# Projecting v for two head groups at once, half of the tokens per job, in a fused attention and mixture-of-experts block

## The chip, the cores and the metric

The kernel runs on one core of one Trainium2 chip. The metric is the device time of one execution in microseconds; 509.33 us is the median of three runs before the change.

## What is computed

There are four batches of 512 tokens with 256 features. The reference, cut to what matters:

```python
def xattn(q, k, v, wq, wk, wv, wo):            # 16 heads of 64, window of 64 keys back
    qh, kh = rope(heads(q @ wq.T)), rope(heads(k @ wk.T))
    vh = heads(v @ wv.T)
    scores = where(window_mask, qh @ kh.T * 64 ** -0.5, -1e30)
    return merge(softmax(scores) @ vh) @ wo.T

x = x + tanh(g_xattn) * xattn(layernorm(x), ctx, ctx, wq, wk, wv, wo)
x = x + tanh(g_ffn) * ffn(layernorm(x), ...)   # 2 shared experts, 16 routed, top 4
```

All large products are made in three float32r products each: every operand is split into a rounded part and a rest (`h` and `l`), and `h*h + h*l + l*h` is summed in PSUM.

## The kernel before

**Units and steps.** Attention is cut into 16 units: unit u is batch u // 4 with the head group g = u % 4 of four heads. A unit has four steps, one per head, so step c is head c % 4 of unit c // 4; 64 steps in all. The list `steps` gives for each step the jobs that are done beside its scores, softmax and transposes, and every engine walks the same list in its own queue. In unit u the q and k of unit u + 1 are projected in steps 4u and 4u + 1, its v in step 4u + 2, and in steps 4u + 1 and 4u + 3 the probabilities are transposed, two heads a time. Job `("v", n)` is the projection of v for unit n, so it stands in step 4n - 2, and ahead of two steps of unit n - 1. The experts follow behind the 64 steps, from about 300 us on.

**Inside TensorE's queue**, an even step begins with the scores of two heads (L1312), goes on with `values` (L1343, probabilities times v, for the pair of heads that was transposed last), and then does its jobs. An odd step has four transposes (L1324) of one head, its jobs, and four transposes of the next. `values(p)` belongs to unit p // 2 and stands in step 2p + 4; the first for unit u therefore stands in step 4u + 4, which is the first step of unit u + 1.

**The v job.** TensorE makes v for four tiles of 128 tokens. Each tile has six products (two halves of the contraction, three products each) with the transposed context as stationary operand and 256 columns of the weight `wh`/`wl` as moving operand, so a job is 24 matmuls of 256 columns into the two PSUM banks of a ring. ScalarE copies both banks (128x1024, L665) to `v_al`, half of which is used for odd, half for even units. SyncE then runs `shift_values`: because a window of 128 keys starts 64 tokens before its block of queries, a second copy `v_sh`, moved by 64 tokens, is made with two DMAs inside SBUF (L369, L370). `values` reads `v_al` for odd blocks of 64 queries and `v_sh` for even ones, and waits for both DMAs through the semaphore `v_in`.

**SyncE's queue** issues all DMAs in the order of `steps`. Behind `shift_values` of an odd unit n stands, in batches 1 and 2 (units 4 and 8, so n = 5 and n = 9), the job `in_scale` (L448): a 256 KB broadcast from DRAM of the scale of the next batch's layer norm into `idle`. GpSimd's job `scale_a` (L540), one step later, waits for it.

**GpSimd's queue** does, besides, the normalisation of the probabilities (`divide`, L521) ahead of the transposes, and half of the rotary embedding (L499 and L502 for q, L508 and L513 for each half of k).

**The weights.** `wh` and `wl` hold 18 slots of 512 floats per partition. The v weights of groups 0 to 3 stand in slots 1, 5, 8 and 12. From the last batch on, expert weights are loaded into slots whose attention weights are done with (`wait_slot_free`).

Of the kernel before, what the change touches and what calls it, by code (L numbers as in the profile page):

```python
# [22 lines left out]
P = 128  # L23
B, L, D = 4, 512, 256
# [40 lines left out]
def build(nc, x_d, xt_d, ctx_d, gx_d, gf_d, w_d, e_d, rw_d, cos_d, sin_d, mask_d, ident_d, out_d):  # L65
    with ExitStack() as ctx:
# [3 lines left out]
        def sem(name):  # L70
# [25 lines left out]
        rw_parts = sb("rw_parts", [P, KC, 2, NR], F32R)  # L96

        sizes = dict(swap=(2, 2, L), qT=(2, 2, L), kT=(2, 2, W + L), idle=(1, 1, L), late=(2, TT, P), spare=(1, 1, 256),
                     v_al=(2, TT, GD), v_sh=(2, TT, GD))
        arena = sb("arena", [P, sum(int(np.prod(s)) for s in sizes.values())])  # L100
        cuts, at = {}, 0
        for name, (a, b, c) in sizes.items():
# [2 lines left out]
        idle = cuts["idle"][:, 0, 0, :]  # L105
        swap = cuts["swap"]
        qT, kT = cuts["qT"], cuts["kT"]
        v_al, v_sh = cuts["v_al"], cuts["v_sh"]
        gate_bc = arena[:, 0:NR * L].rearrange("p (e n) -> p e n", e=NR)
        sneg_a = sb("sneg", [P, 2, TT, P])  # L110
        sneg = [sneg_a[:, 0, :, :], sneg_a[:, 1, :, :], cuts["late"][:, 0, :, :], cuts["late"][:, 1, :, :]]
# [194 lines left out]

            return j if j < 2 else j - B + 2

        def fillings(u):

            return u // 2 + 1

        def side(j):

# [13 lines left out]
        def wait_slot_free(eng, i):  # L328

            if i >= NE:  # L330
                kind, g = ORDER[slot(i)]
                eng.wait_ge(y_pe if kind == "y" else v_pe, (B - 1) * GROUPS + g + 1)

        def gated_parts(n):

# [18 lines left out]
        def _(sp):  # L354
# [8 lines left out]
                sp.wait_ge(c_lo, b + 1)  # L363
                sp.dma_start(craw[:, :, :], ctx_d[b]).then_inc(in_ctx, 16)

            def shift_values(u):

                sp.wait_ge(v_out, u + 1)
                sp.dma_start(v_sh[W:P, u % 2, :, :], v_al[0:W, u % 2, :, :]).then_inc(v_in[u % 2], 16)  # L369
                sp.dma_start(v_sh[0:W, u % 2, 1:TT, :],  # L370
                             v_al[W:P, u % 2, 0:TT - 1, :]).then_inc(v_in[u % 2], 16)

            def move(dst, blocks, done):

# [223 lines left out]
        def _(act):  # L598
# [45 lines left out]
            def do(job):  # L644
                kind, n = job
                if kind == "w":
                    act.wait_ge(in_raw[n % RAW], 16 * (n // RAW + 1))
                    wait_slot_free(act, n)
                    act.activation(wh[:, slot(n), :], raw[:, n % RAW, :], ACT.Copy).then_inc(w_hi, 1)
                elif kind == "ctx" and n == 0:  # L650
                    for kc in range(KC):
                        act.wait_ge(in_ctx0[kc], 16)
                        act.activation(xTh[1][:, kc, :], craw[:, kc, :], ACT.Copy).then_inc(c_hi, 1)
                elif kind == "ctx":
                    act.wait_ge(in_ctx, 16 * n)
                    act.wait_ge(v_pe, GROUPS * n)
                    act.activation(xTh[1][:, :, :], craw[:, :, :], ACT.Copy).then_inc(c_hi, 1)
                elif kind == "xT":
                    round_bank_pair(xTh[side(n)], job, xT_pe, xT_hi)
                elif kind == "v":  # L660
                    act.wait_ge(v_pe, n + 1)
                    if n >= 2:
                        act.wait_ge(oT_pe, 2 * (n - 1))
                        act.wait_ge(v_in[n % 2], 32 * (fillings(n) - 1))
                    act.activation(v_al[:, n % 2, :, :].rearrange("p t d -> p (t d)"),  # L665
                                   both_banks(job)[:, :, :].rearrange("p a n -> p (a n)"),
                                   ACT.Copy).then_inc(v_out, 1)
                elif kind == "expert":
                    expert(n)
                elif kind == "rexp":  # L670
                    act.wait_ge(r_sub, n + 1)
                    act.activation(lexp[:, :, :], lex[:, :, :], ACT.Exp).then_inc(r_exp, 1)
                elif kind == "xhi":
                    X = side(B + n)
                    act.wait_ge(xn_moved, 256 * (n - 1))
                    act.wait_ge(up_pe, NE * (n - 1))
                    act.wait_ge(r_pe, n - 1)
                    act.activation(xTh[X][:, :, :], xnT, ACT.Copy).then_inc(xT_hi, 1)
                elif kind == "xhi_d":
                    act.wait_ge(x_shifted, n - 1)  # L680
                    act.wait_ge(qk_pe[0], GROUPS * n + 1)
                    act.activation(xTh[0][:, :, :], xd, ACT.Copy).then_inc(xT_hi, 1)
                elif kind in ("norm_a", "norm_b"):
                    normalise(n, kind)
# [440 lines left out]
        def _(pe):  # L1125
# [79 lines left out]
            def do(job):  # L1205
# [16 lines left out]
                elif kind in "qk":  # L1222
                    b, g = divmod(n, GROUPS)
                    i = PIECE_OF[kind, g]
                    weights(i)
                    if kind == "q":
                        pe.wait_ge(xT_lo, b + 1)
                    else:
                        pe.wait_ge(c_lo, b + 2)
                    X = 0 if kind == "q" else 1  # L1230
                    for half in range(2):
                        for kc in range(KC):
                            last = product(two[half], [cols(i, kc * D + half * P, P)],
                                           [(xTh[X][:, kc, :], xTl[X][:, kc, :])],
                                           start=kc == 0, stop=kc == KC - 1)
                        if (kind, n) == ("q", 0) or half:
                            last.then_inc(qk_pe["qk".index(kind)], 1)
                elif kind == "v":
                    b, g = divmod(n, GROUPS)
                    i = PIECE_OF["v", g]  # L1240
                    weights(i)
                    pe.wait_ge(c_lo, b + 2)
                    for t in range(TT):
                        last = product(two[t // 2][:, (t % 2) * GD:(t % 2 + 1) * GD],
                                       [(xTh[1][:, kc, t * P:(t + 1) * P],
                                         xTl[1][:, kc, t * P:(t + 1) * P]) for kc in range(KC)],
                                       [cols(i, kc * D, D) for kc in range(KC)])
                    last.then_inc(v_pe, 1)
                elif kind == "y":
                    i = PIECE_OF["y", n % GROUPS]  # L1250
                    weights(i)
                    pe.wait_ge(oT_lo, 2 * (n + 1))
                    for t in range(TT):
                        last = product(two[t // 2][:, (t % 2) * D:(t % 2 + 1) * D],
                                       [(oTh[:, j, t * P:(t + 1) * P], oTl[:, j, t * P:(t + 1) * P])
                                        for j in range(2)],
                                       [cols(i, j * D, D) for j in range(2)])
                    last.then_inc(y_pe, 1)
                elif kind == "r" and n in FULL_ROUTER:
                    pe.wait_ge(xn_moved, 256 * (n - 1))  # L1260
                    for kc in range(KC):
                        for t in range(TT):
                            last = pe.matmul(two[0][QUAD * t:QUAD * t + NR, 0:P], rw[:, kc, :],
                                             xnT[:, kc, t * P:(t + 1) * P], start=kc == 0, stop=kc == KC - 1)
                    last.then_inc(r_pe, 1)
                elif kind == "r":
                    pe.wait_ge(rw_lo, 1)
                    pe.wait_ge(xT_lo, B + n + 1)
                    X = side(B + n)

                    for kc in range(KC):
                        for part in (xTh[X], xTl[X]):
                            last = pe.matmul(two[0][0:2 * NR, :], rw_parts[:, kc, :, :].rearrange("p a e -> p (a e)"),
                                             part[:, kc, :], start=kc == 0 and part is xTh[X],
                                             stop=kc == KC - 1 and part is xTl[X])
                    last.then_inc(r_pe, 1)
# [50 lines left out]
            def values(p):  # L1327
# [1 line left out]
                u, pair = divmod(p, 2)  # L1329
                pe.wait_ge(p_out, 2 * p + 2)  # L1330
                if pair == 0:
                    pe.wait_ge(v_out, u + 1)
                    pe.wait_ge(v_in[u % 2], 32 * fillings(u))
                if p:
                    pe.wait_ge(oT_lo, p)
                else:
                    pe.wait_ge(pool_init, 1)
                for blk in range(L // W):
                    t, e = divmod(blk, 2)
                    v = v_al if e else v_sh  # L1340
                    for h in range(2):
                        head = 2 * pair + h
                        last = pe.matmul(psO[h * DH:(h + 1) * DH, blk * W:(blk + 1) * W],  # L1343
                                         v[:, u % 2, t, head * DH:(head + 1) * DH],
                                         pT[:, (2 * p + h) % 4, t, e * W:(e + 1) * W],
                                         start=True, stop=True)
                last.then_inc(oT_pe, 1)
# [109 lines left out]
```

## Time and profile before

| | |
|---|---|
| median of three runs | 509.33 us (509.26 to 509.49) |
| the profiled execution, its own time | 508.84 us |
| its span in the trace | 507.1 us |
| TensorE busy | 496.7 us, 98% |
| VectorE, ScalarE, GpSimd busy | 358.2, 310.9, 267.3 us |
| granted TensorE clock, mean | 0.999 |

The busy time of an engine is the union of its instructions. Matmuls overlap each other in the trace by their fill and drain, so what a matmul costs is read from the distance between the starts of two, and not from its duration. A unit of attention takes about 17.5 us in the middle of the run. GpSimd's 53% is a mean over a first part in which it is nearly always busy and the experts, where it hardly works.

### The profile page before, as it was taken

To read this page: it belongs to the slowest core of one execution; us is meant where nothing else is said; L and a number is where in the kernel's file an instruction comes from. 1 tells how busy PE (TensorE), PEld (TensorE's weight loads), DVE (VectorE), ACT (ScalarE), POOL (GpSimd) and SP (SyncE) were. 2 spreads that over 40 slices of the span, in tenths; PEclk is the share of its full clock that TensorE was granted. 3 is DMA by queue.
4 is the path that set the end of the run, shared out by engine and by line. 5 is a ranking of instruction groups with operands and counts; after the bars stand their busy time and mean duration, and the time that the engine had idled before them with its cause. 6 is when DMAs were issued, how large, how long until landed. Compare 5 with 4: busy or idle time off the path is not lost.

```text
span 507.1 us, 14396 instructions
## 1 busy us (share of the span) xinstructions
PE 496.7 (98%) x5426; PEld 417.6 (82%) x5426; DVE 358.2 (71%) x1159; ACT 310.9 (61%) x861; POOL 267.3 (53%) x206
## 2 busy tenths in 40 slices
PE   8998999999999999999999999999999999999997
PEld 5778888889988998888888788777878887888885
DVE  6989858665787667768877768786657565745454
ACT  5595785656766665865767765766456545644442
POOL 4999999899997999997888511001000100000000
PEclk9999999999999999999999999999999999999999
DMA  8462124121212210220221146315812680256021
GB/s 268 121 202 80 44 67 135 44 80 38 57 67 71 71 38 24 59 59 23 59 59 27 35 160 247 95 25 145 276 16 31 172 248 10 32 148 238 1 34 49
DMA packets 49363, 46.36 MB, mean 91 GB/s; under 512 B 29936, under 2 KB 32368, under 8 KB 49296
## 3 DMA queue, kind: packets, MB, share of 16 engines
q1 hardware_dynamic: 49296, 45.46, 31.2%
q8 instruction: 43, 0.70, 0.6%
q14 instruction: 24, 0.20, 0.2%
HBM read 32.72 MB, written 2.24 MB: 69 GB/s over the span
## 4 chain that ended last, share of the span: by engine, by line
PE 76%; POOL 13%; DVE 5%; issue 4%; DMA 1%; ACT 1%; SPq 0%; DVEq 0%; POOLq 0%; ACTq 0%
PE ring L1131 54%; PE psS L1131 10%; PE psO L1343 5%; POOL arena L508 4%; PE psT L1324 4%; PE psS L1312 3%; POOL arena L513 3%; POOL prob L521 2%; POOL wl L529 2%; DVE arena L1026 1%; DVE wl L946 1%; POOL arena L502 1%; DVE arena L859 1%; DMA raw<-in_w 1%; POOL arena L499 1%
## 5 line engine op out<-in xcount | busy, mean ns | idle before, releaser
L1131 PE MATMUL ring<-xTh,wh 128*128 128x512 f32 x268 | 108.2, 404 | 0.5 <-DVE lex L888 0.2
L1131 PE MATMUL ring<-xTh,wl 128*128 128x512 f32 x268 | 105.3, 393 | 0.0
L1131 PE MATMUL ring<-xTl,wh 128*128 128x512 f32 x268 | 105.1, 392 | 0.0
L632 ACT ACTIVATE oTh<-prob 128x512 fp32r<-128x512 f32 x64 | 40.4, 631 | 54.3 <-PE ring L1131 26.8
L521 POOL TENSOR_TENSOR prob<-prob,rinv 128x512 f32<-128x512 f32 x62 | 66.8, 1078 | 12.6 <-DVE rinv L1036 12.4
L929 DVE TENSOR_TENSOR oTl<-prob,oTh 128x512 fp32r<-128x512 f32 x64 | 44.1, 689 | 37.1 <-ACT oTh L632 36.7
L555 POOL TENSOR_TENSOR rstd<-vare,mhalf 128x4 f32<-128x4 f32 x8 | 9.7, 1214 | 103.1 <-DVE vare L826 103.1
L616 ACT ACTIVATE sneg<-ring 128x512 f32<-128x512 f32 x72 | 42.8, 595 | 33.2 <-PE ring L1131 33.1
L921 DVE TENSOR_TENSOR prob<-sneg,arena 128x512 f32<-128x512 f32 x64 | 44.2, 690 | 24.9 <-ACT sneg L616 24.8
L1131 PEld LDWEIGHTS ring<-xTh,wh 128*128 128x128 f32 x268 | 50.4, 188 | 13.0 <-issue 1.3
L1131 PEld LDWEIGHTS ring<-xTh,wl 128*128 128x128 f32 x268 | 50.3, 188 | 11.2
L1131 PEld LDWEIGHTS ring<-xTl,wh 128*128 128x128 f32 x268 | 50.4, 188 | 10.5
L723 ACT ACTIVATE pT<-psT 128x512 f32<-128x512 f32 x64 | 38.0, 593 | 33.6 <-PE psT L1324 33.4
L707 ACT ACTIVATE prob<-arena,nmax 128x128 f32<-128x128 f32 x128 | 49.7, 394 | 12.2 <-DVE nmax L1026 12.2
L707 ACT ACTIVATE prob<-sneg,nmax 128x128 f32<-128x128 f32 x128 | 49.6, 391 | 7.4 <-DVE nmax L1026 7.3
L513 POOL TENSOR_TENSOR arena<-arena 128x512 f32<-128x512 f32 x37 | 49.0, 1324 | 2.7
L508 POOL TENSOR_TENSOR arena<-arena,sin 128x512 f32<-128x512 f32 x37 | 50.1, 1353 | 0.0
L856 DVE STREAM_SHUFFLE arena<-ring 128x512 f32<-128x512 f32 (+1 forms) x51 | 45.7, 897 | 0.2
L859 DVE TENSOR_TENSOR arena<-ring,cos 128x512 f32<-128x512 f32 (+1 forms) x51 | 41.2, 808 | 0.0
L1131 PE MATMUL ring<-wh,oTh 128*128 128x256 f32 x128 | 37.4, 292 | 2.0 <-DVE oTl L1040 1.8
L1324 PE MATMUL psT<-ident,prob 128*128 128x128 f32 x256 | 38.7, 273 | 0.4 <-ACT pT L723 0.2
L962 DVE SCALAR_TENSOR_TENSOR x<-ring,tg,x 128x1024 f32<-128x1024 f32 x16 | 20.5, 1278 | 25.9 <-PE ring L1131 25.9
(144 smaller groups left out, 1221.9 us busy)
## 6 DMA issues: line engine op xcount, KB each, us to landing
arena<-gate_scratch SPq DMA_DIRECT2D x64, 256.0 KB, 6.1
raw<-in_e SPq DMA_DIRECT2D x18, 256.0 KB, 2.6
raw<-in_w SPq DMA_DIRECT2D x16, 256.0 KB, 3.7
arena<-arena SPq DMA_DIRECT2D x16, 256.0 KB, 3.1
arena<-arena SPq DMA_DIRECT2D x16, 192.0 KB, 3.5
pT<-pT SPq DMA_DIRECT2D x96, 32.0 KB, 2.0
out<-x SPq DMA_DIRECT2D x16, 128.0 KB, 5.8
x<-in_x SPq DMA_DIRECT2D x3, 512.0 KB, 4.7
```

What stands on the lines that cost most here:

```text
L508: link(pool.tensor_tensor(part, part, sin[:, :], ALU.mult))
L513: pool.tensor_tensor(dst, dst, swap[:, i, pair, :], ALU.add).then_inc(qk_rot[i], 1)
L521: pool.tensor_tensor(prob[:, c % BUFS, :, :], prob[:, c % BUFS, :, :], rinv[:, c % BUFS, :].unsqueeze(2).to_broadcast([P, TT, P]), ALU.mul ...
L616: act.activation(act_g[:, n % 2, :], ring[0][:, n % 2, :], ACT.Gelu).then_inc(f_gelu, 1)
L632: act.activation(gated_parts(n)[0], src, ACT.Copy).then_inc(f_hi, 1)
L707: last = act.activation(prob[:, c % BUFS, t, :], sneg[c % BUFS][:, t, :], ACT.Exp, bias=nmax[:, c % 4, t:t + 1], scale=-1.0, accum_out=rsu ...
L856: dve.stream_shuffle(swap[:, i, pairs, :], part, [(lane + QUAD // 2) % QUAD for lane in range(QUAD)]).then_inc(qk_swap[i], 1)
L859: dve.tensor_tensor(dst[:, pairs, :], part, cos[:, :].unsqueeze(1).to_broadcast(part.shape), ALU.mult).then_inc(qk_mul[i], 1)
L921: dve.tensor_tensor(act_f[:, n % 4, :], act_g[:, n % 2, :], gate_bc[:, r, :], ALU.mult).then_inc(f_mul, 1)
L929: dve.tensor_tensor(lo, src, hi.bitcast(F32), ALU.subtract).then_inc(f_lo, 1)
L1131: last = pe.matmul(out, a, b, start=start and i == 0 and j == 0, stop=stop and i == n - 1 and j == 2, skip_group_check=check)
L1324: last = pe.transpose(psT[:, t, :], prob[:, c % BUFS, t, :], ident[:, :])
```

## The change

For the first batch (units 0 to 3) nothing changes but the places of v in `v_al`. For units 4 to 15, the v jobs of an even unit u and of u + 1 are shared out anew: job u makes token tiles 0 and 1 for both units, job u + 1 makes tiles 2 and 3 for both. Each product then has 512 moving columns, two runs of 256 that lie 4 slots (8 KB per partition) apart, so a job is 12 matmuls of 512 columns. `v_al` grows from 8 to 10 tiles, with places chosen by `values_at`. ScalarE's copy has the same size and is written as two runs of two tiles. `shift_values` has two DMAs for an even job (128 KB and 64 KB) and five for an odd one: two that complete `v_sh` of the even unit (128 KB each) and three for the odd unit (256, 128 and 64 KB). An even unit's `values` must now wait for the odd job behind it.

```diff
+        def values_at(u, t):
+            if u % 2 == 0:
+                return t
+            if u >= GROUPS and t < 2 and u // 2 % 2 == 0:
+                return TT + t
+            return TT + 2 + t
+        def halves(at, skip, rows):
+            wide = cuts_from_v[rows, at * GD:(at + 2 * skip) * GD]
+            return wide.rearrange("p (h r) -> p h r", h=2)[:, :, 0:2 * GD]
+        def shifted(u):
+            moves = [2 if n < GROUPS else 4 - n % 2 for n in range(u % 2, u + 1, 2)]
+            return 16 * sum(moves)
...
-            def shift_values(u):
-                sp.wait_ge(v_out, u + 1)
-                sp.dma_start(v_sh[W:P, u % 2, :, :], v_al[0:W, u % 2, :, :]).then_inc(v_in[u % 2], 16)
-                sp.dma_start(v_sh[0:W, u % 2, 1:TT, :],
-                             v_al[W:P, u % 2, 0:TT - 1, :]).then_inc(v_in[u % 2], 16)
+            def shift_values(n):
+                sp.wait_ge(v_out, n + 1)
+                a = values_at(n, 0)
...
+                elif n % 2 == 0:
+                    sp.dma_start(v_sh[W:P, 0, 0:2, :], v_al[0:W, 0:2, :]).then_inc(v_in[0], 16)
+                    sp.dma_start(v_sh[0:W, 0, 1, :], v_al[W:P, 0, :]).then_inc(v_in[0], 16)
+                else:
+                    sp.dma_start(v_sh[W:P, 0, 2:TT, :], v_al[0:W, 2:TT, :]).then_inc(v_in[0], 16)
+                    sp.dma_start(v_sh[0:W, 0, 2:TT, :], v_al[W:P, 1:TT - 1, :]).then_inc(v_in[0], 16)
+                    skip = values_at(n, 2) - a
+                    sp.dma_start(v_sh[W:P, 1, :, :].rearrange("p (h t) d -> p h (t d)", h=2),
+                                 halves(a, skip, slice(0, W))).then_inc(v_in[1], 16)
+                    sp.dma_start(v_sh[0:W, 1, 1:3, :], v_al[W:P, a:a + 2, :]).then_inc(v_in[1], 16)
+                    sp.dma_start(v_sh[0:W, 1, 3, :], v_al[W:P, a + skip, :]).then_inc(v_in[1], 16)
...
+                    if n >= GROUPS:
+                        if n % 2 == 0:
+                            act.wait_ge(v_in[1], shifted(n - 3))
+                        at = values_at(n - n % 2, n % 2 * 2)
+                        skip = values_at(n - n % 2 + 1, n % 2 * 2) - at
+                        act.activation(halves(at, skip, slice(0, P)).rearrange("p u (t d) -> p u t d", t=2),
+                                       both_banks(job)[:, :, :].rearrange("p t (u d) -> p u t d", u=2),
+                                       ACT.Copy).then_inc(v_out, 1)
...
+                    if b:
+                        both = slice(PIECE_OF["v", g - g % 2], PIECE_OF["v", g - g % 2 + 1] + 1,
+                                     PIECE_OF["v", g - g % 2 + 1] - PIECE_OF["v", g - g % 2])
+                        for half in range(2):
+                            t = g % 2 * 2 + half
+                            last = product(two[half],
+                                           [(xTh[1][:, kc, t * P:(t + 1) * P],
+                                             xTl[1][:, kc, t * P:(t + 1) * P]) for kc in range(KC)],
+                                           [(wh[:, both, kc * D:(kc + 1) * D],
+                                             wl[:, both, kc * D:(kc + 1) * D]) for kc in range(KC)])
...
                 if pair == 0:
-                    pe.wait_ge(v_out, u + 1)
-                    pe.wait_ge(v_in[u % 2], 32 * fillings(u))
+                    pe.wait_ge(v_out, u + 1 if u < GROUPS else u // 2 * 2 + 2)
+                    pe.wait_ge(v_in[u % 2], shifted(u))
```

## Rows read from the trace of the kernel before

**Rows 1.** The page's head: the span, and each engine's busy time, share, instructions.

```profile
span 507.1 us, 14396 instructions
PE 496.7 (98%) x5426; PEld 417.6 (82%) x5426; DVE 358.2 (71%) x1159; ACT 310.9 (61%) x861; POOL 267.3 (53%) x206
```

**Rows 2.** The chain that ended last, in order of time: start us, us, what.

```profile
84.24 1.01 POOL prob L521
...
204.50 0.59 DVE oTl L1040
...
258.56 0.59 DVE oTl L1040
...
273.44 3.06 PE ring L1131 x24
```

**Rows 3.** Timeline of TensorE in unit 8: start us, us, instruction.

```profile
157.88 0.50 PE L1131 MATMUL ring<-xTh,wh 128*128 128x512 f32 x1
...
160.75 0.60 PE L1324 MATMUL psT<-ident,prob 128*128 128x128 f32 x4
...
166.47 0.38 PE L1131 MATMUL ring<-wh,xTh 128*128 128x256 f32 x1
166.70 0.28 PE L1131 MATMUL ring<-wl,xTh 128*128 128x256 f32 x1
...
169.32 0.28 PE L1131 MATMUL ring<-wh,xTl 128*128 128x256 f32 x1
169.44 0.60 PE L1324 MATMUL psT<-ident,prob 128*128 128x128 f32 x4
```

**Rows 4.** Timeline of ScalarE in unit 4: the copy of v.

```profile
99.65 1.03 ACT L665 ACTIVATE arena<-ring 128x1024 f32<-128x1024 f32 x1 [0.29 <-PE ring L1131]
```

**Rows 5.** Timeline of SyncE's DMA issues: start us, us, line.

```profile
100.70 0.47 SPq L369 DMA_DIRECT2D arena<-arena  x1
101.21 0.60 SPq L370 DMA_DIRECT2D arena<-arena  x1
101.86 0.61 SPq L448 DMA_DIRECT2D arena<-norm_scratch  x1
...
242.22 0.46 SPq L369 DMA_DIRECT2D arena<-arena  x1
```

**Rows 6.** DMA issues by kind: count, KB each, median us from issue to landing.

```profile
arena<-arena SPq DMA_DIRECT2D x16, 256.0 KB, 3.1
arena<-arena SPq DMA_DIRECT2D x16, 192.0 KB, 3.5
pT<-pT SPq DMA_DIRECT2D x96, 32.0 KB, 2.0
...
arena<-norm_scratch SPq DMA_DIRECT2D x4, 256.0 KB, 3.3
```

**Rows 7.** Timeline of TensorE: values of units 4 and 12, a transpose of unit 5.

```profile
104.22 1.15 PE L1343 MATMUL psO<-pT,arena 128*64 128x64 f32 x32
...
120.18 0.60 PE L1324 MATMUL psT<-ident,prob 128*128 128x128 f32 x4
...
245.66 1.15 PE L1343 MATMUL psO<-pT,arena 128*64 128x64 f32 x32
```

**Rows 8.** Timeline of GpSimd behind the scale's load.

```profile
104.52 1.04 POOL L521 TENSOR_TENSOR prob<-prob,rinv 128x512 f32<-128x512 f32 x1
105.52 1.56 POOL L540 TENSOR_TENSOR xn<-xn,arena 128x512 f32<-128x512 f32 x1
...
109.90 2.40 POOL L499 TENSOR_TENSOR arena<-arena,sin 128x1024 f32<-128x1024 f32 x1 [0.32 <-DVE arena L856]
...
118.33 1.04 POOL L521 TENSOR_TENSOR prob<-prob,rinv 128x512 f32<-128x512 f32 x1
```

More of the change, by code:

```diff
@@ L98, in build @@
         sizes = dict(swap=(2, 2, L), qT=(2, 2, L), kT=(2, 2, W + L), idle=(1, 1, L), late=(2, TT, P), spare=(1, 1, 256),
-                     v_al=(2, TT, GD), v_sh=(2, TT, GD))
+                     v_al=(1, 5 * KC, GD), v_sh=(2, TT, GD))
         arena = sb("arena", [P, sum(int(np.prod(s)) for s in sizes.values())])
@@ L107, in build @@
         qT, kT = cuts["qT"], cuts["kT"]
-        v_al, v_sh = cuts["v_al"], cuts["v_sh"]
+        v_al, v_sh = cuts["v_al"][:, 0, :, :], cuts["v_sh"]
+        v_start = sum(int(np.prod(sizes[name])) for name in sizes if name not in ("v_al", "v_sh"))
+        cuts_from_v = arena[:, v_start:at]
         gate_bc = arena[:, 0:NR * L].rearrange("p (e n) -> p e n", e=NR)
@@ L307, in by_pe @@
             return j if j < 2 else j - B + 2
-        def fillings(u):
-            return u // 2 + 1
+        def values_at(u, t):
[10 more added lines that the diff above has]
+            return 16 * sum(moves)
         def side(j):
@@ L331, in wait_slot_free @@
                 kind, g = ORDER[slot(i)]
-                eng.wait_ge(y_pe if kind == "y" else v_pe, (B - 1) * GROUPS + g + 1)
+                if kind == "v":
+                    eng.wait_ge(v_pe, (B - 1) * GROUPS + g // 2 * 2 + 2)
+                else:
+                    eng.wait_ge(y_pe if kind == "y" else v_pe, (B - 1) * GROUPS + g + 1)
         def gated_parts(n):
@@ L364, in load_ctx @@
                 sp.dma_start(craw[:, :, :], ctx_d[b]).then_inc(in_ctx, 16)
-            def shift_values(u):
-                sp.wait_ge(v_out, u + 1)
-                sp.dma_start(v_sh[W:P, u % 2, :, :], v_al[0:W, u % 2, :, :]).then_inc(v_in[u % 2], 16)
-                sp.dma_start(v_sh[0:W, u % 2, 1:TT, :],
-                             v_al[W:P, u % 2, 0:TT - 1, :]).then_inc(v_in[u % 2], 16)
+            def shift_values(n):
+                sp.wait_ge(v_out, n + 1)
+                a = values_at(n, 0)
+                if n < GROUPS:
+                    sp.dma_start(v_sh[W:P, n % 2, :, :], v_al[0:W, a:a + TT, :]).then_inc(v_in[n % 2], 16)
+                    sp.dma_start(v_sh[0:W, n % 2, 1:TT, :],
+                                 v_al[W:P, a:a + TT - 1, :]).then_inc(v_in[n % 2], 16)
+                elif n % 2 == 0:
+                    sp.dma_start(v_sh[W:P, 0, 0:2, :], v_al[0:W, 0:2, :]).then_inc(v_in[0], 16)
+                    sp.dma_start(v_sh[0:W, 0, 1, :], v_al[W:P, 0, :]).then_inc(v_in[0], 16)
+                else:
+                    sp.dma_start(v_sh[W:P, 0, 2:TT, :], v_al[0:W, 2:TT, :]).then_inc(v_in[0], 16)
[5 more added lines that the diff above has]
+                    sp.dma_start(v_sh[0:W, 1, 3, :], v_al[W:P, a + skip, :]).then_inc(v_in[1], 16)
             def move(dst, blocks, done):
@@ L663, in do @@
                         act.wait_ge(oT_pe, 2 * (n - 1))
[L664 to L667, printed above, removed]
+                        act.wait_ge(v_in[n % 2], shifted(n - 2))
+                    if n >= GROUPS:
[6 more added lines that the diff above has]
+                                       ACT.Copy).then_inc(v_out, 1)
+                    else:
+                        at = values_at(n, 0)
+                        act.activation(v_al[:, at:at + TT, :].rearrange("p t d -> p (t d)"),
+                                       both_banks(job)[:, :, :].rearrange("p a n -> p (a n)"),
+                                       ACT.Copy).then_inc(v_out, 1)
                 elif kind == "expert":
@@ L1242, in do @@
                     pe.wait_ge(c_lo, b + 2)
-                    for t in range(TT):
+                    if b:
[8 more added lines that the diff above has]
+                                             wl[:, both, kc * D:(kc + 1) * D]) for kc in range(KC)])
+                    for t in range(TT if b == 0 else 0):
                         last = product(two[t // 2][:, (t % 2) * GD:(t % 2 + 1) * GD],
@@ L1339, in values @@
                     t, e = divmod(blk, 2)
-                    v = v_al if e else v_sh
+                    v = v_al[:, values_at(u, t), :] if e else v_sh[:, u % 2, t, :]
                     for h in range(2):
@@ L1343, in values @@
                         last = pe.matmul(psO[h * DH:(h + 1) * DH, blk * W:(blk + 1) * W],
-                                         v[:, u % 2, t, head * DH:(head + 1) * DH],
+                                         v[:, head * DH:(head + 1) * DH],
                                          pT[:, (2 * p + h) % 4, t, e * W:(e + 1) * W],
```

## The prediction

> **What bounds the kernel now.** I read the page's head first [rows 1]: TensorE is busy for 496.7 of 507.1 us, so a saving on it can reach the end, and a new wait on it certainly does. Then the chain of waits in the stretch of batches 1 to 3 [rows 2], because a saving in one job counts only where the chain runs through that job. Up to 85 us the chain runs through GpSimd's divisions; from there to about 199 us it is TensorE without a break; between 199 and 259 us it leaves TensorE four times and comes back each time through VectorE's rest of the attention output, `oTl`, for which the y job waits (the first and the last of the four returns are shown); at 273.44 us the last v job is on it again. Then I read the timeline of TensorE inside one unit for the price of a v job [rows 3], and the timelines of the four engines behind a v job (ScalarE's copy, SyncE's issues, the values, GpSimd) for what hangs on its end [rows 4, 5, 7, 8].
>
> **The matmuls.** Twelve jobs change (units 4 to 15). A v job of 24 matmuls with 256 columns goes from 166.47 to 169.44 us, 2.97 us; a q or k job of 12 with 512 columns, which also stands right behind values, goes from 157.88 to 160.75 us, 2.87 us [rows 3]. Both have the same number of columns, and 12 fewer starts are worth 0.10 us. So the new job should take 2.87 us, and the whole edit saves 12 x 0.10 = 1.2 us at the very most. The trace shows no matmul whose moving operand has two runs 8 KB apart. Its cost lies between nothing (then the q job's 2.87 holds) and the start that was saved (then 2.97 stays and nothing is won); a run within one instruction has no decoding and no weight load of its own, so I take nothing.
>
> A rule weighed against this: inside the job a 256-column matmul follows the other by (169.32 - 166.70) / 22 = 0.119 us [rows 3], which is 12 ns above 256 columns at 2.4 GHz. The Trainium skill's page "TensorE: Matmul & The Clock Gate", section "Back-to-back issue gap", gives columns over the clock plus about 2.5 ns for a lone matmul, by which 144 starts fewer would be worth 0.36 us in all and not 1.2. The measured distance decides.
>
> **Which of the twelve savings are on the chain.** By [rows 2], job 4 (about 80 us) lies where GpSimd ends the wait, and jobs 11, 12, 13 and 14 lie within the four detours over VectorE, which start at the k job and end at `oTl`; a shorter v job there only makes the y job wait 0.1 us longer. Left are jobs 5 to 10 and 15: 7 x 0.10 = 0.7 us.
>
> **ScalarE's copy.** Same size, 1.03 us [rows 4], written in two runs of 512 floats; I take no change. Its wait on the reader before is the same count as now, since values for unit n - 2 stand ahead of the job in the same step. The bigger arena costs only memory.
>
> **The wait that gets shorter cover: values of an even unit.** Before, v of unit u was ready a whole unit ahead. Now unit u (even, from 4) needs job u + 1, in step 4u + 2, and its values are in step 4u + 4. The first issue stands at 100.70 and the values start at 104.22 us: 3.52 us; for unit 12 it is 245.66 - 242.22 = 3.44 us [rows 5, 7]. Units 6, 8 and 10 lie between these; unit 14 has 8 more transposes in front and more room. The shorter v job moves both ends alike. The values need the first two transfers, 128 KB each. From [rows 6]: 32 KB land after 2.0 us, 256 KB after 3.1, so about (3.1 - 2.0) / 224 = 4.9 ns per KB and 2.5 us for 128 KB. The second is issued 0.51 us behind the first [rows 5], so it lands at 0.51 + 2.5 = 3.0 us; with something for the transfers behind it, 3.1 to 3.2. That is inside 3.44 by about 0.3 us, so I price it at nothing. From above: today's second transfer lands 3.5 us behind its own issue, with 192 KB and 256 KB in front [rows 6], which would be 0.51 + 3.5 = 4.0 and a TensorE stall of 0.5 us in five units, 2.6 us. By size the new pair (256 KB together against 448) is nearer the lower figure.
>
> The page "DMA: Bandwidth & Descriptors" of the Trainium skill gives about 2.0 us plus the bytes at 436 GB/s per transfer; that is 2.3 us for 128 KB and a landing at 2.8. It agrees that nothing is late, by a little more.
>
> **What is pushed back in SyncE's queue.** An odd job issues five DMAs in the place of two. At 0.51 to 0.65 us each [rows 5], three more are about 1.85 us. Behind them, for jobs 5 and 9, stands the load of the layer norm scale. It is issued at 101.86 now and lands, by its median of 3.3, at 105.2 us; GpSimd takes it at 105.52 [rows 6, 8], 0.3 us later, with no gap behind the division that ends at 105.56. In the changed kernel it is issued at about 103.6 (101.86 + 1.85 - 0.1 for the shorter job) and lands at 103.6 + 3.4 = 107.0, 1.5 us after GpSimd wants it. It could be 1.1 (a landing 0.4 us quicker) or 2.0 (it queues behind 704 KB instead of 448).
>
> What is late next: GpSimd's queue is full, and behind `scale_a` stand a division, `scale_b` and the next q's rotation, which has 0.32 us of idle time in front [rows 8]. So 1.5 - 0.32 = 1.2 us are left. The division of head 21 then ends at 118.33 + 1.04 + 1.2 = 120.57, and its transposes start at 120.18 today [rows 7]. With 0.05 us for the signal TensorE starts them at 120.62: +0.44 us, and the savings of jobs 5 and 6, which lie before, are swallowed. In the next unit GpSimd's lag falls below the slack of the divisions, so it doesn't repeat until job 9, where the rows have the same distances to the hundredth: +0.44 again, swallowing jobs 9 and 10.
>
> **Sum.** 2 x 0.44 - 3 x 0.10 (jobs 7, 8, 15) = +0.6 us. From the profiled execution's own 508.84 us (its span is 507.1) that is 509.4; that execution lies 0.49 below the median of the runs, so against the median I predict 509.9 us.
>
> **The rivals.**
>
> *The v landing is late (chance 0.22).* The mechanism: two issues and two landings no longer fit between job u + 1 and values of unit u. It decides from a landing later than 3.44 to 3.52 us behind the first issue; at 3.7 it costs 5 x 0.2 = 1.0 us, at 4.0 2.6 us. For it: today's second transfer takes 3.5 us by itself. Against it: the sizes. A TensorE stall also gives GpSimd its time back, so the two losses don't add fully. Time: 510.5 to 512.1. This is the case that ends slower.
>
> *Everything is hidden (0.27).* The scale's load lands by 106.6 or GpSimd's lag falls under the 0.8 us that the division has, and only the saving is seen: -0.7 us, 508.6. Should jobs 4 and 11 to 14 count as well, it is -1.2 and 508.1. For it: each slack is only missed by some tenths.
>
> *The wide matmul isn't cheaper (0.07).* If the second run costs a start, the job stays at 2.97 and the sum is +0.9: 510.2. If it costs more than that, each 10 ns more on 144 instructions are 1.4 us.
>
> My forecast has the remaining 0.44, between 509.2 and 510.6, as GpSimd's wait is 1.1 to 2.0 us.
>
> **How the numbers follow.** Within 0.2% is 508.3 to 510.35 us, about what a measurement of this kernel tells from no change. Faster needs nearly all twelve savings and no wait: 0.07. Slower takes nearly all of the first rival, a fifth of my forecast (a wait near 2 us) and part of the third: 0.31. No change that can be told: 0.62. The range reaches from the hidden case, 508.5, to most of the late landing, 511.8.
>
> **What the profile of the changed kernel would show.** Right: v jobs of 12 matmuls and 2.87 us; the issue of the scale's load about 3.0 us behind the first of five; GpSimd idle for 1.1 to 2.0 us in front of `scale_a` in units 4 and 8, released by that DMA; TensorE idle for some tenths in front of transposes at about 120 and 190 us, released by GpSimd; no idle time in front of values of even units. Wrong: idle time there, released by the DMAs of v, in five units (the first rival); no gap on GpSimd (the second); a v job of 2.97 us or more (the third).

## The result and the profile after

The changed kernel takes 513.86 us (median of 5 runs, 513.11 to 514.36) against 509.49 us for the kernel before in the same session; the ratio is 1.0077, with a 95% interval of 1.0064 to 1.0089. It is 0.8% slower, 3.9 us by the ratio. The prediction was 509.9 us with a range of 508.5 to 511.8, so it was wrong: the direction was right and the mechanism was the one that it named, but one term, GpSimd's wait for the load of the scale, was put at 1.5 us and was 2.7 to 2.8.

The page's head, to be held against [rows 1]:

```profile
span 512.0 us, 14132 instructions
PE 497.2 (97%) x5282; PEld 409.6 (80%) x5282; DVE 358.9 (70%) x1159; ACT 311.0 (61%) x861; POOL 266.9 (52%) x206
```

TensorE has 144 instructions fewer, a span 4.9 us longer, and next to no more busy time: what was added is waiting. What it is comes from the waits in total (engine, what waited, for what: us in all, times, longest; the lists are cut). First TensorE's, then GpSimd's:

```profile
PE psT L1376 <- POOL prob L553: 3.0, 3, 1.5
PE ring L1173 <- DVE oTl L1082: 2.7, 5, 0.8
PE psS L1190 <- POOL arena L521: 1.3, 1, 1.3
```

```profile
...
POOL xn L572 <- DMA arena<-norm_scratch: 5.5, 2, 2.8
```

GpSimd waits twice, 5.5 us in all, for the load of the layer norm scale; before, it never did. TensorE's list before has no wait for a division, and 1.8 us for `oTl`. Nothing in its list after is released by a DMA of v. Around unit 4 the timelines say how that happens. SyncE's issues, against [rows 5]:

```profile
101.57 0.47 SPq L397 DMA_DIRECT2D arena<-arena  x1
102.08 0.60 SPq L398 DMA_DIRECT2D arena<-arena  x1
102.72 0.66 SPq L400 DMA_DIRECT2D arena<-arena  x1
103.42 0.61 SPq L402 DMA_DIRECT2D arena<-arena  x1
104.07 1.62 SPq L403 DMA_DIRECT2D arena<-arena  x1
105.74 0.58 SPq L480 DMA_DIRECT2D arena<-norm_scratch  x1
```

GpSimd, against [rows 8]; the number in brackets is idle time and what ended it:

```profile
105.50 1.05 POOL L553 TENSOR_TENSOR prob<-prob,rinv 128x512 f32<-128x512 f32 x1
109.34 1.56 POOL L572 TENSOR_TENSOR xn<-xn,arena 128x512 f32<-128x512 f32 x1 [2.79 <-DMA arena<-norm_scratch]
...
113.37 2.37 POOL L531 TENSOR_TENSOR arena<-arena,sin 128x1024 f32<-128x1024 f32 x1
```

TensorE, against [rows 3, 7]: the wide v job and the transposes behind it, values of unit 4, and two waits.

```profile
97.44 0.50 PE L1173 MATMUL ring<-wh,xTh 128*128 128x512 f32 x1
...
100.32 0.60 PE L1376 MATMUL psT<-ident,prob 128*128 128x128 f32 x4
...
105.09 1.15 PE L1395 MATMUL psO<-pT,arena 128*64 128x64 f32 x32
...
119.26 0.66 PE L1376 MATMUL psT<-ident,prob 128*128 128x128 f32 x4 [1.47 <-POOL prob L553]
...
122.86 0.66 PE L1376 MATMUL psT<-ident,prob 128*128 128x128 f32 x4
...
191.22 0.66 PE L1376 MATMUL psT<-ident,prob 128*128 128x128 f32 x4 [1.40 <-POOL prob L553]
```

The reader is to see four things. The v job takes 100.32 - 97.44 = 2.88 us. The load's issue stands 105.74 - 101.57 = 4.17 us behind the first of the five. GpSimd stands still for 2.79 us, and the 0.32 us that it had in front of the next q's rotation are gone. Some 10 us later TensorE waits 1.47 us for a division, and in unit 9 (191.22 us) 1.40 us.

To see where the time goes without adding up waits, I compare the starts of the first values of each pair with those in the kernel before (after minus before, us): first values of the run +0.94, unit 4 +0.87, unit 5 +2.74, second values of unit 6 +3.08, unit 8 +2.89, unit 9 +4.71, unit 10 +5.05, unit 15 +4.95. So there are two steps of 1.87 and 1.81 us, two small ones of 0.44 and 0.35 us behind them (units 6 and 10), and slow gains of about 0.1 us a unit between. The 0.94 us at the start lie ahead of every edit; the other kernels below show between 0.49 and 1.92 us there, also those that leave v untouched, so I put them down to the execution and not to the change.

### The profile page after: what moved, and what is told of

It reads as the page before. It is cut to its first block, busy times and chain, and to the rows that moved or that the text cites. A ratio compares the mean times of both kernels' runs of the same rounds, so it can differ in the third digit from the quotient of the medians.

```text
span 512.0 us, 14132 instructions
## 1 busy us (share of the span) xinstructions
PE 497.2 (97%) x5282; PEld 409.6 (80%) x5282; DVE 358.9 (70%) x1159; ACT 311.0 (61%) x861; POOL 266.9 (52%) x206
## 4 chain that ended last, share of the span: by engine, by line
PE 65%; POOL 19%; DVE 6%; issue 5%; DMA 2%; SPq 1%; ACT 1%; DVEq 0%; POOLq 0%; ACTq 0%
PE ring L1173 45%; PE psS L1173 10%; POOL prob L553 5%; POOL arena L540 4%; POOL arena L545 3%; PE psO L1395 3%; PE psT L1376 2%; PE psS L1364 2%; POOL arena L534 2%; POOL arena L531 2%; DMA arena<-norm_scratch 2%; PE psS L1190 1%; DVE arena L901 1%; DVE arena L898 1%; DVE arena L1068 1%
```

## The experiments

Theory A: the loss is the scale's load, pushed back in SyncE's queue by the three more transfers of the odd job. Rival B: the transfers or the new places of v cost by themselves. Ratios are to the kernel before, run on the same chip in the same session, with the 95% interval in brackets; offsets are those of the starts of values against the trace of the kernel before, as above, and rest on one trace of each kernel.

**The load ahead of the v job.**

```diff
-                jobs.append((spread[k, g], b + 1))
+                jobs.insert(0 if spread[k, g] == "in_scale" else len(jobs), (spread[k, g], b + 1))
```

> The changed kernel with one edit: in SyncE's queue the load of the layer norm scale stands ahead of the v job of its step, not behind its five DMAs. Theory A (the loss is the scale's load pushed back, 2.8 and 2.7 us of GpSimd waiting, 1.87 and 1.81 us on TensorE): both waits vanish, the kernel falls by 3.7 us and what follows from them (0.4 us in unit 6), to 509 to 510 us, ratio to before 0.998 to 1.001. Rival B (the five transfers or the new places of v cost by themselves, through contention): it stays above 512 us.

509.83 us, ratio 1.0003 (0.9994 to 1.0012): the whole loss is gone. The load is issued at 93.74 us, when its own wait for the stored scale ends:

```profile
93.74 0.32 SPq L480 DMA_DIRECT2D arena<-norm_scratch  x1
...
103.89 1.57 SPq L403 DMA_DIRECT2D arena<-arena  x1
```

```profile
105.28 1.03 POOL L553 TENSOR_TENSOR prob<-prob,rinv 128x512 f32<-128x512 f32 x1
106.27 1.55 POOL L572 TENSOR_TENSOR xn<-xn,arena 128x512 f32<-128x512 f32 x1
...
110.59 2.40 POOL L531 TENSOR_TENSOR arena<-arena,sin 128x1024 f32<-128x1024 f32 x1 [0.26 <-DVE arena L898]
```

GpSimd goes straight from the division to the scaling and has its idle time in front of the rotation back. All five transfers are still issued, one of them with the same long issue of 1.57 us, and they cost nothing that shows: rival B falls. From unit 3 on the offset goes from +0.76 to +0.27, a gain of 0.5 us.

**Transfers pushed into the kernel before.** Constants are copied into a tile `extra` that nobody reads; its declaration and its semaphore are left out here.

```diff
...
+                if u in (5, 9):
+                    if u == 9:
+                        sp.wait_ge(extra_in, 48)
+                    sp.dma_start(extra[W:P, :, :],
+                                 cos[0:W, :].unsqueeze(1).to_broadcast([W, 2, L])).then_inc(extra_in, 16)
+                    sp.dma_start(extra[0:W, 0, :], cos[W:P, :]).then_inc(extra_in, 16)
+                    sp.dma_start(extra[0:W, 1, 0:D], mask[W:P, :, :].rearrange("p a c -> p (a c)")).then_inc(extra_in, 16)
```

> The kernel before, with three transfers of 256, 128 and 64 KB inside SBUF (constants into an unused tile) issued between the shift of v for units 5 and 9 and the load of the scale; nothing of v is changed, the extra tile is not read. Theory A: GpSimd waits 2.5 to 3 us for the scale in units 4 and 8 and the kernel is 3 to 4 us slower than before, about 513 us. Rival B: no change, under 510 us.

514.56 us, ratio 1.0101 (1.0088 to 1.0115). With v untouched, three transfers in this place make the whole loss and 1 us more: GpSimd waits longer (3.19 and 3.08 us), and no v job is shorter. GpSimd's waits:

```profile
POOL xn L550 <- DMA arena<-norm_scratch: 6.3, 2, 3.2
```

**The price of the wide matmul.** As the first run, with narrow products again:

```diff
-                            last = product(two[half],
-                                           [... for kc in range(KC)],
-                                           [(wh[:, both, kc * D:(kc + 1) * D],
-                                             wl[:, both, kc * D:(kc + 1) * D]) for kc in range(KC)])
+                            for j in range(2):
+                                last = product(two[half][:, j * GD:(j + 1) * GD],
+                                               [... for kc in range(KC)],
+                                               [cols(PIECE_OF["v", g - g % 2 + j], kc * D, D) for kc in range(KC)])
```

> As the run with the scale's load first, but each product of 512 columns is again two of 256, 24 matmuls per v job; sharing out of the tokens, transfers and places as in the changed kernel. The prediction's price: 2.97 us per job against 2.87, of twelve jobs seven on the chain, so this one is 0.7 us slower than the run with the scale first; 1.2 us if all twelve count; 0 if GpSimd sets the pace.

510.23 us, ratio 1.0013 (1.0004 to 1.0021), against 509.83 (1.0003): 0.4 us more in the medians, with intervals that just overlap. The traces are sharper. This kernel's offset is +1.81 in unit 3 and +1.88 in unit 15, no gain at all; the wide one gained 0.5 us over the same stretch. A v job of this kernel, from its first matmul to the transposes behind it:

```profile
98.29 0.39 PE L1173 MATMUL ring<-wh,xTh 128*128 128x256 f32 x1
...
101.27 0.60 PE L1376 MATMUL psT<-ident,prob 128*128 128x128 f32 x4
```

It is 2.98 us. The wide job takes 2.88 us in the changed kernel and 2.90 us in the run with the load first, and the q jobs there 2.83 to 2.88. So the second run 8 KB away costs at most some hundredths of a microsecond in twelve matmuls.

**The pair for the even unit late.** As the first run, with the 256 KB transfer issued ahead of the two that values wait for:

```diff
+                    skip = values_at(n, 2) - a
+                    sp.dma_start(v_sh[W:P, 1, :, :]..., halves(a, skip, slice(0, W))).then_inc(v_in[1], 16)
                     sp.dma_start(v_sh[W:P, 0, 2:TT, :], v_al[0:W, 2:TT, :]).then_inc(v_in[0], 16)
                     sp.dma_start(v_sh[0:W, 0, 2:TT, :], v_al[W:P, 1:TT - 1, :]).then_inc(v_in[0], 16)
-                    skip = values_at(n, 2) - a
-                    sp.dma_start(v_sh[W:P, 1, :, :]..., halves(a, skip, slice(0, W))).then_inc(v_in[1], 16)
```

> As the run with the scale's load first, but the 256 KB transfer for the odd unit is issued ahead of the two 128 KB transfers that the even unit's values wait for. In the changed kernel these land 2.8 us behind the first issue, 0.7 us ahead of values. With 0.65 us for the issue and 1.1 us for the data in front, the second lands at about 4.5 us, 1.0 us late, in five units: 4 to 5 us slower than the run with the scale first. If GpSimd or VectorE were the true bound, under 1 us.

518.04 us, ratio 1.0173 (1.0158 to 1.0189), 8.2 us above the first run; expected were 4 to 5. TensorE's waits and the first of them:

```profile
PE psO L1395 <- DMA arena<-arena: 7.4, 5, 2.4
```

```profile
107.01 1.51 PE L1395 MATMUL psO<-pT,arena 128*64 128x64 f32 x32 [2.37 <-DMA arena<-arena]
```

The prediction's first rival is real and ready: one transfer in front is enough. The run is a miss in size, and two things make it. The first wait is 2.37 us and the other four are 1.06 to 1.35 us, where 1.0 was expected. And behind the first one, with TensorE idle for 2.37 us ahead of it, the granted clock was 0.50 from about 108 to 111 us, its lower level of 1.2 GHz; matmuls of 512 columns start 0.43 us apart there and 0.23 us apart behind it:

```profile
109.05 0.63 PE L1173 MATMUL ring<-xTl,wh 128*128 128x512 f32 x1
109.48 0.63 PE L1173 MATMUL ring<-xTh,wl 128*128 128x512 f32 x1
...
111.59 0.39 PE L1173 MATMUL ring<-xTh,wl 128*128 128x512 f32 x1
111.82 0.39 PE L1173 MATMUL ring<-xTh,wh 128*128 128x512 f32 x1
```

From the first to the second values of unit 4 the offset grows by 1.55 us (+2.79 to +4.34) with no wait in between: that is the price of the low clock. Behind the four shorter waits, and behind the waits of 1.4 to 1.6 us in the changed and in the pushed kernel, it stayed at 1.00. Why the first wait is 1 us longer than the others stays open.

In the changed kernel the same two land 2.2 and 2.3 us behind their issues, the later at 102.08 + 2.3 = 104.4, 0.7 us ahead of values at 105.09.

**Which part of a transfer in front counts: its issue or its bytes?** Two variants of the pushed kernel, again in units 5 and 9 only. Three transfers of 4 KB:

```diff
+                    sp.dma_start(extra[W:P, 0, 0:16], cos[0:W, 0:16]).then_inc(extra_in, 16)
+                    sp.dma_start(extra[0:W, 0, 0:16], cos[W:P, 0:16]).then_inc(extra_in, 16)
+                    sp.dma_start(extra[0:W, 1, 0:16], cos[W:P, 16:32]).then_inc(extra_in, 16)
```

> The kernel before with three transfers of 4 KB each in front of the scale's load for units 5 and 9: three more issues, hardly any bytes. If the issues alone carry the delay, as the prediction had it, the load is issued about 3.0 us behind the first and lands 3.4 later, GpSimd waits 1.6 us, and TensorE loses about 0.5 us twice: 510 to 511 us. If the bytes count besides, this wait is clearly shorter than the 3.2 us of the run with 448 KB pushed in: the load's own landing stays at 3.4 us here and was 4.4 there.

514.18 us, ratio 1.0086 (1.0071 to 1.0101). Nearly the same loss with hardly any bytes:

```profile
102.33 0.47 SPq L371 DMA_DIRECT2D arena<-arena  x1
...
104.86 0.60 SPq L379 DMA_DIRECT2D extra<-cos  x1
105.50 0.58 SPq L456 DMA_DIRECT2D arena<-norm_scratch  x1
```

```profile
109.97 1.56 POOL L549 TENSOR_TENSOR xn<-xn,arena 128x512 f32<-128x512 f32 x1 [2.77 <-DMA arena<-norm_scratch]
...
181.26 1.54 POOL L549 TENSOR_TENSOR xn<-xn,arena 128x512 f32<-128x512 f32 x1 [2.03 <-DMA arena<-norm_scratch]
```

The load is issued 3.17 us behind the first, as the prediction's sum for issues has it (3.0). But it lands after 4.3 us in unit 4 and 3.5 in unit 8, where 3.4 was expected for both.

One transfer of 448 KB:

```diff
+                    sp.dma_start(extra[:, :].rearrange("p (a c) -> p a c", a=2),
+                                 cos[:, 0:448].unsqueeze(1).to_broadcast([P, 2, 448])).then_inc(extra_in, 16)
```

> The kernel before with one transfer of 448 KB in front of the scale's load for units 5 and 9: one more issue, all the bytes. If issues alone count, the load is issued 0.65 us later, lands before or just when GpSimd wants it, no loss. If bytes count: 448 KB at 0.2 MB per us are 2.2 us more in front of it, its landing stretches from 3.4 to about 5 us, GpSimd waits 2 us or more and the kernel is 2 us or more slower than before.

511.57 us, ratio 1.0043 (1.0026 to 1.0060). The load is issued 1.91 us behind the first and takes 4.3 us to land:

```profile
101.79 0.47 SPq L371 DMA_DIRECT2D arena<-arena  x1
...
103.70 0.66 SPq L455 DMA_DIRECT2D arena<-norm_scratch  x1
```

```profile
108.17 1.54 POOL L548 TENSOR_TENSOR xn<-xn,arena 128x512 f32<-128x512 f32 x1 [1.55 <-DMA arena<-norm_scratch]
```

Both count. Three issues with hardly any bytes make a wait of 2.0 to 2.8 us, all the bytes with one issue 1.5 us, both together 3.1 to 3.2 us; they don't add. What it is in a small transfer that stretches a later landing isn't shown: the three still touch 64 partitions each, and none with fewer was run.

**The load between the second and the third transfer.**

```diff
-                jobs.append((spread[k, g], b + 1))
+                if spread[k, g] != "in_scale":
+                    jobs.append((spread[k, g], b + 1))
...
+                    if n in (5, 9):
+                        do(("in_scale", n // GROUPS + 1))
                     skip = values_at(n, 2) - a
```

> The changed kernel with the scale's load issued between the second and the third transfer of the odd job, where it stood before relative to them. Theory A: its landing is back at about 4.6 us behind the first issue, GpSimd doesn't wait, and the time is that of the run with the scale first, within 0.3 us, 4 us under the changed kernel. If the number of transfers around it mattered and not its place, GpSimd would still wait 1 us or more.

511.07 us, ratio 1.0026 (1.0011 to 1.0042). A miss: the load is issued 1.15 us behind the first, just where it stood in the kernel before, and GpSimd still waits:

```profile
102.40 0.47 SPq L398 DMA_DIRECT2D arena<-arena  x1
102.91 0.60 SPq L399 DMA_DIRECT2D arena<-arena  x1
103.55 0.59 SPq L483 DMA_DIRECT2D arena<-norm_scratch  x1
```

```profile
POOL xn L575 <- DMA arena<-norm_scratch: 2.0, 2, 1.3
```

Its landing takes 5.0 us in unit 4 and 4.4 in unit 8. So the transfers issued behind it slow it too. In this kernel the offset grows from +1.79 in unit 3 to +2.30 in unit 15, where it falls by 0.5 us with the load first. So of the 4.5 us between the changed kernel (+0.96 to +4.95) and the one with the load first, the place in the queue explains 3.5, and the company of the transfers behind it 1.0.

**The places in memory.** The kernel before with a gap ahead of `v_sh`:

```diff
-                     v_al=(2, TT, GD), v_sh=(2, TT, GD))
+                     v_al=(2, TT, GD), gap=(1, 2, GD), v_sh=(2, TT, GD))
```

> The kernel before with nothing changed but the place of v_sh in memory, 512 floats per partition further on, as the larger v_al of the changed kernel puts it. The changed kernel's trace is 0.94 us late already at the first values of unit 0, which no edit of unit 4 or later explains. If the places cause it, this kernel is 0.5 to 1 us slower than before; if the start merely varies from run to run, no difference, within 0.1%.

510.34 us, ratio 1.0001 (0.9991 to 1.0011): no difference. Its trace has an offset of +1.92 at the first values and +1.82 in unit 15, so the start varies by more than 1 us from execution to execution with no effect on the comparison of medians.

## Why the prediction was wrong, step by step

**The matmuls: right.** 2.97 us fell to 2.88 a job (2.90 in the run with the load first), 0.07 to 0.09 where 0.10 was taken; narrow products in the changed order give 2.98. The smaller saving that was weighed against it, 0.36 us in all or 0.03 a job, is refuted by the same rows.

**Which savings are on the chain: right, to the job.** With the load first the offset falls by 0.07 to 0.09 us across each of the jobs 5 to 10 and 15, the seven that were named, 0.5 us in all (0.7 had been taken, at 0.10 each). Units 10 to 13 show the expected standstill: +0.36 in unit 10 and +0.34 in unit 13, since the y job waits longer for `oTl` instead. But it is a finding of the traces. The 0.4 us between the medians with wide and with narrow products point the same way, with intervals that overlap; and against the kernel before, the interval of 0.9994 to 1.0012 leaves no room for a whole 0.5 us (0.9990).

**ScalarE's copy and values of an even unit: right.** No wait of values on a DMA appears. The landing was put at 3.0 to 3.2 us behind the first issue and was 0.51 + 2.3 = 2.8, so the slack is 0.7 us and not 0.3. The page "DMA: Bandwidth & Descriptors" of the Trainium skill gives, in the section "Anatomy of one DMA — SWDGE (gpsimd) path", 2.0 us plus the bytes at 436 GB/s. That is a fit to transfers issued by GpSimd, and these are SyncE's; the estimate from it was 2.8 us all the same, and the trace agrees. For the load of 256 KB the same fit gives an estimate of 2.6 us. Measured were 3.4 to 5.0 us with other transfers around it, and the measurement decides: what fits each of two transfers in front says little about one in a row of six.

**What is pushed back in SyncE's queue: the step that failed, by the size of GpSimd's wait.** The prediction had the load issued about 3.0 us behind the first transfer, landing 3.4 us later, and GpSimd waiting 1.5 us, with 1.1 to 2.0 as bounds. Measured were 2.79 and 2.68 us. In unit 4 the issue came 4.17 us behind the first, as the fifth transfer took 1.62 us to issue, and the landing took 3.5; in unit 8 the issue came at 176.85 - 173.59 = 3.26 us and the landing took 4.3:

```profile
173.59 0.47 SPq L397 DMA_DIRECT2D arena<-arena  x1
...
176.85 0.53 SPq L480 DMA_DIRECT2D arena<-norm_scratch  x1
```

The error was to price a transfer in the queue at its issue time alone and to carry over the landing time of a load with two transfers in front and none behind it. Why one and the same row of transfers spends its extra microsecond once on the issue and once in the landing, and why three transfers of 4 KB stretch a later landing at all, stays open. Single long issues aren't bound to this row: in the kernel before, the load of `xn` took 1.57 us to issue at 161.03 us, and 0.43 us in the changed kernel.

**What is late next: right, but for 0.1 to 0.2 us.** The prediction had TensorE's loss as GpSimd's wait less 0.32 us of idle time, less 0.81 of slack, plus 0.05: wait - 1.08. Over all runs, by the step of the offsets from unit 4 to 5 and from 8 to 9:

| kernel | GpSimd's wait, us | wait - 1.08 | TensorE's loss |
|---|---|---|---|
| changed | 2.79, 2.68 | 1.71, 1.60 | 1.87, 1.81 |
| three transfers pushed in | 3.19, 3.08 | 2.11, 2.00 | 2.17, 2.04 |
| three tiny transfers | 2.77, 2.03 | 1.69, 0.95 | 1.76, 0.98 |
| one of 448 KB | 1.55, 1.47 | 0.47, 0.39 | 0.49, 0.47 |
| load third | 1.28, 0.72 | 0.20, none | 0.39, -0.09 |

A wait of 1.5 us costs 0.47 to 0.49 us, and 0.44 were forecast. Above the point where it binds, every tenth of the wait is a tenth on TensorE, twice. The formula is 0.02 to 0.08 us low where the v job is narrow, since the transposes behind a wait take 0.66 us and not 0.60. It is 0.16 to 0.21 low where the job is wide: there TensorE was about 0.1 us ahead of GpSimd by the shorter job (105.09 - 104.22 = 0.87 us late, GpSimd 105.50 - 104.52 = 0.98), and gave that back. So 1.2 us more of waiting and these 0.2 make 2 x 1.4 us of the miss.

The place needs a word. The prediction named the transposes of head 21 (120.18 us before). Those of head 20 have more slack, 1.11 us in the kernel before:

```profile
114.72 1.03 POOL L521 TENSOR_TENSOR prob<-prob,rinv 128x512 f32<-128x512 f32 x1
...
116.86 0.60 PE L1324 MATMUL psT<-ident,prob 128*128 128x128 f32 x4
```

With a wait of 2.8 us on GpSimd they are late too and take the first part, the 1.47 us at 119.26; head 21 adds the last 0.3 (its transposes start at 122.86, right behind the division that ends at 122.81) and sets the total, as forecast.

**"It doesn't repeat": wrong by a little.** There is a second, smaller loss in each batch, 0.44 us in unit 6 and 0.35 in unit 10. The prediction had GpSimd's lag fall below the slack in the next unit, and nothing behind it. In unit 6 it is a job held by GpSimd's rest of the context, which was still behind; in unit 10 the y job's wait for `oTl` is 0.80 us where it was 0.36:

```profile
146.77 0.47 PE L1173 MATMUL ring<-xTh,wh 128*128 128x512 f32 x1 [0.54 <-POOL xTl L566]
...
210.28 0.36 PE L1173 MATMUL ring<-wh,oTh 128*128 128x256 f32 x1 [0.80 <-DVE oTl L1082]
```

Both links are read from the traces alone. The same small steps (0.26 to 0.44 us) are in all kernels in which GpSimd waits for the load, also in unit 10 of the one with the load third, where unit 9 had lost nothing; neither is there when the load is first (0.08 and 0.00 us).

**The sum.** 1.87 + 1.81 + 0.44 + 0.35 - 0.5 = 4.0 us, against 3.9 by the ratio; the prediction had 2 x 0.44 - 0.3 = 0.6. Of the 3.4 us between them, 2.8 are the two steps, whose cause was tested, and 0.8 the second losses, less 0.2 for more savings than were counted.

**The rivals.** Everything hidden: refuted in this kernel, and true of the waits once the load goes first. The landing of v late: didn't happen, 0.7 us away. The wide matmul not cheaper: refuted.

No version beat the kernel before beyond doubt. The one with the load first equals it at 1.0003; its saving of 0.5 us is seen in the trace, and not in the times.

## What to carry to other kernels

When a change adds DMAs to a queue, look for the transfer behind them whose consumer has the least slack, and put it ahead if its own inputs are ready: here moving one issue gave back the whole loss. Don't price a queued DMA by its issue time alone, nor a landing by one that was measured with other neighbours; bound it by an experiment that pushes dummy transfers in front of it. And a saving on an engine that is 98% busy is worth only the share of jobs that the chain of waits really runs through, here seven jobs of twelve, and even their 0.5 us couldn't be told in the times.

## What the runs showed of the hardware

- Three transfers of 4 KB ahead of a load of 256 KB delayed what waits for it by 2.0 to 2.8 us; one of 448 KB by 1.5 us. Small transfers aren't cheap neighbours.
- The same load of 256 KB landed after 3.4 us with two transfers in front and none behind, 5.0 and 4.4 with two in front and three behind, 4.3 with three in front (one of them 448 KB), and 3.5 to 4.5 behind five.
- The fifth transfer of five in a row took 1.62 us to issue in unit 4 of the changed kernel and 0.48 to 0.68 us in its other units.
- A moving operand in two runs of 256 columns, 8 KB apart, runs at nearly the speed of 512 columns in one: 2.88 to 2.90 us for 12 such matmuls, the q jobs' 2.83 to 2.88.
- Behind 2.37 us in which TensorE stood still, its granted clock was 0.50 for about 3 us and the work there took 1.55 us longer; behind waits of 1.06 to 1.62 us it stayed at 1.00.
